# One layer of attention, RWKV mixing and two feed-forward blocks in float32: two scales moved to ScalarE, sums moved from VectorE to adding DMAs, one more sum begun in PSUM

## The reference, cut to what matters

```
x = x + attention(layernorm(x))          # (xn Wq^T)(xn^T xn), no softmax
x = x + ffn(layernorm(x))                # f1
x = rwkv(x):  x = x + time_mix(ln1(x));  x = x + channel_mix(ln2(x))
x = x + ffn(layernorm(x))                # f2, the same weights as f1

ffn(y):  z = y + relu(y W1 + b1) W2 + b2         # the router's weight is 1 for expert 0
         return (z - mean(z)) * rsqrt(var(z) + eps) * gamma + beta
```

## Time and profile before

| | |
|---|---|
| median of 3 runs | 262.93 us (262.4 to 263.28) |
| the profiled execution | 264.55 us |
| its span, first to last instruction | 262.8 us |
| TensorE busy | 253.0 us (96%) |
| VectorE busy | 232.7 us (89%) |
| ScalarE busy | 227.4 us (87%) |
| GpSimd busy | 153.1 us (58%) |

### The profile page before, as it was taken

One profiled execution on the slowest core, in us unless ns is written; L12 is line 12 of the kernel. 1 busy time (PEld: TensorE's weight loads), 2 busy tenths in 40 slices (PEclk: granted clock), 3 DMA queues, 4 the chain that ended last, 5 costly groups with the idle time before them and its releaser, 6 DMA issues.

```text
span 262.8 us, 5291 instructions
## 1 busy us (share of the span) xinstructions
PE 253.0 (96%) x1508; PEld 189.6 (72%) x1508; DVE 232.7 (89%) x762; ACT 227.4 (87%) x439; POOL 153.1 (58%) x290
## 2 busy tenths in 40 slices
PE   7999999999999999999999999999999999999991
PEld 6877686778777686667677767757874977777771
DVE  4598699999999999999999999999999987816384
ACT  1589899988988999899999999999999999993640
POOL 4558788832984774657927166964817158353522
PEclk9999999999999999999999999999999999999997
DMA  7922202402024220222403142063222526450332
GB/s 204 300 90 41 41 2 41 80 0 42 1 44 80 40 40 4 40 41 42 81 1 60 22 80 42 1 115 69 50 49 49 110 46 108 94 114 12 64 96 80
DMA packets 16908, 16.53 MB, mean 63 GB/s; under 512 B 1392, under 2 KB 11504, under 8 KB 16880
## 3 DMA queue, kind: packets, MB, share of 16 engines
q0 software_dynamic: 5616, 10.23, 22.9%
q1 hardware_dynamic: 10848, 5.84, 8.0%
q10 hardware_dynamic: 416, 0.14, 0.2%
HBM read 3.87 MB, written 2.10 MB: 23 GB/s over the span
## 4 chain that ended last, share of the span: by engine, by line
PE 84%; ACT 4%; POOL 4%; issue 3%; DVE 3%; DMA 1%; DVEq 0%; ACTq 0%; POOLq 0%
PE bank L1117 19%; PE bank L1126 19%; PE bank L1188 10%; PE bank L1194 8%; PE bank L1076 7%; PE bank L1089 3%; PE bank L1104 3%; PE bank L1169 3%; PE bank L1164 3%; PE bank L1205 2%; PE bank L1175 2%; PE bank L1159 2%; PE bank L1237 1%; DMA R<-in_hidden 1%; ACT f_h L907 1%
## 5 line engine op out<-in xcount | busy, mean ns | idle before, releaser
L1126 PEld LDWEIGHTS bank<-W,f_h 128*128 128x128 f32 x480 | 59.0, 192 | 12.0 <-issue 11.0
L1117 PE MATMUL bank<-f_yT,W 128*128 128x512 f32 x128 | 63.3, 595 | 0.0
L1126 PE MATMUL bank<-W,f_h 128*128 128x128 f32 x480 | 60.8, 275 | 0.0
L1194 PEld LDWEIGHTS bank<-FWv,KK 128*128 128x128 f32 x256 | 30.9, 192 | 3.4 <-issue 2.6
L1194 PE MATMUL bank<-FWv,KK 128*128 128x128 f32 x256 | 32.2, 276 | 0.0
L1188 PE MATMUL bank<-XK,FWk 128*128 128x512 f32 x64 | 30.5, 596 | 0.8 <-ACT KK L964 0.6
L1117 PEld LDWEIGHTS bank<-f_yT,W 128*128 128x128 f32 x128 | 21.2, 191 | 12.4 <-issue 7.8
L840 ACT ACTIVATE f_y<-R,f_yn_nb,f_yn_rs 128x128 f32<-128x128 f32 x64 | 26.3, 484 | 3.3 <-POOL f_yn_nb L350 3.1
L907 ACT ACTIVATE f_h<-bank,B1C 128x512 f32<-128x512 f32 x36 | 24.3, 686 | 0.2 <-PE bank L1126 0.2
L907 ACT ACTIVATE f_h<-bank,B 128x512 f32<-128x512 f32 x28 | 18.6, 681 | 6.0 <-PE bank L1126 3.3
L293 POOL TENSOR_TENSOR f_yn_ve<-f_yn_mv,K_EPS 128x4 f32<-128x4 f32 x16 | 7.3, 457 | 25.1 <-DVE f_yn_mv L529 25.1
(11 more groups left out here) (160 smaller groups left out, 637.2 us busy)
## 6 DMA issues: line engine op xcount, KB each, us to landing
R<-BETA POOLq DMA_DIRECT2D x16, 256.0 KB, 3.4
R<-f_zg POOLq DMA_DIRECT2D x11, 256.0 KB, 3.4
R<-N POOLq DMA_DIRECT2D x8, 256.0 KB, 3.7
R<-in_hidden SPq DMA_DIRECT2D x7, 256.0 KB, 5.6
out_x<-R SPq DMA_DIRECT2D x7, 256.0 KB, 2.3
R<-G POOLq DMA_DIRECT2D x4, 256.0 KB, 3.5
W<-in_w SPq DMA_DIRECT2D x2, 256.0 KB, 5.1
BETA<-in_beta SPq DMA_DIRECT2D x1, 256.0 KB, 5.2
```

What stands on the lines that cost most here:

```text
L1117: t_.matmul(banks[bank][:], W1[:, n * P:(n + 1) * P], at(f.yT, b)[:], start=True, stop=True).then_inc(f.h_psum[n], 1)
L1126: last = t_.matmul(banks[bank][:, j * C:(j + 1) * C], at(f.h, b)[:, n, j * P:(j + 1) * P], W2[:, n, :], start=False, stop=(n == H - 1), sk ...
L1194: last = t_.matmul(banks[bank][:, j * C:(j + 1) * C], at(KK, b)[:, n, j * P:(j + 1) * P], FWv[:, n, :], start=(n == 0 and j == 0), stop=(n ...
```

## The change

The change has four parts.

1. **First tile.** `first_shift` and `first_power` leave GpSimd. ScalarE does the same with a logarithm (bias eps) and an exponential (scale -0.5). TensorE now begins with `attn_transpose(0)`, whose first two parts read only the first half, and `attn_gram(0)` follows. `bias_rows` moves from behind `attn_proj(0)` to behind `attn_gram(2)`.
2. **Last tile.** `last_shift` and `last_power` become `last_log` and `last_root` on ScalarE, at the end of its list. `last_scaled(0)` moves ahead of `last_mean_var(0)`.
3. **Sums.** `ffn_add` is removed: the sums of `f1` tile 4 and of `f2` tiles 5 and 6 become `ffn_sum` on GpSimd. `cmix_out` stays for tile 7 alone: tiles 0, 1 and 6 become `cmix_sum`. `f2` tile 4 joins `STARTED`, so one `ffn_start` leaves TensorE and one comes to VectorE.
4. **Order and banks.** All four lists are written anew, with other banks. TensorE's has 127 calls with a wait for a bank where it had 135.

`z_log` and `z_root` are defined, and nothing calls them. The core of the diff (the lists are cut to their ends):

```diff
-ADDED = {"f1": (0, 4), "f2": (5, 6, 7), "x3": (0, 1, 6, 7)}
+ADDED = {"f1": (0,), "f2": (7,), "x3": (7,)}
 SPLIT = {"f1": (0,), "f2": (7,)}
-STARTED = {"f1": (0, 1, 2, 3), "f2": (5, 6, 7)}
+STARTED = {"f1": (0, 1, 2, 3), "f2": (4, 5, 6, 7)}
...
@@ gpsimd
-            first_shift(0); first_power(0); first_shift(1); first_power(1); shift(1, na); power(1, na); bias(1, na)
+            shift(1, na); power(1, na); bias(1, na); shift(2, na); power(2, na); bias(2, na); shift(3, na)
...
+            ffn_sum(4, f1, f1.zg); ffn_residual(5, f1); shift(1, ncm); power(1, ncm); back_scale(2); bias(1, ncm)
...
-            z_shift(6, f2); power(6, f2.znorm); last_shift(0); last_power(0); last_shift(1); last_power(1)
+            power(5, f2.znorm); ffn_residual(7, f2); ffn_sum(5, f2, f2.zg); z_shift(6, f2); power(6, f2.znorm)
+            ffn_sum(6, f2, f2.zg)
@@ vector
-            warm_tile(); first_stats(0); first_mean_var(0); first_stats(1); first_mean_var(1); attn_stats(1)
-            first_normed(0); first_normed(1); bias_diagonal(); mean_var(1, na); attn_stats(2); attn_stats(3)
+            warm_tile(); first_stats(0); first_mean_var(0); first_stats(1); first_mean_var(1); first_normed(0)
+            first_normed(1); attn_stats(1); mean_var(1, na); attn_stats(2); mean_var(2, na); attn_stats(3)
...
-            ffn_scaled(6, f2, 6); ffn_add(6, f2, f2.zg); last_stats(0, 5); last_mean_var(0); last_stats(1, 3)
-            last_mean_var(1); last_scaled(0, 5); last_scaled(1, 3); last_out(0); last_out(1)
+            ffn_scaled(5, f2, 1); z_stats(6, f2, 3); mean_var(6, f2.znorm); ffn_scaled(6, f2, 3); last_stats(0, 0)
+            last_scaled(0, 0); last_mean_var(0); last_stats(1, 2); last_mean_var(1); last_scaled(1, 2); last_out(0)
+            last_out(1)
@@ scalar
+            def log_rows(n, rows, wait, b, done):
+                act.wait_ge(*wait)
+                if b >= 2:
+                    act.wait_ge(f2.zg_ready, b - 1)
+                c = slice(rows[0], rows[-1] + 1)
+                a.activation(n.ve[b % 2][:, c], n.mv[b % 2][:, c, 1], ACT.Ln, bias=K_EPS[:, 0:1]).then_inc(done, 1)
+            def root_rows(n, rows, wait, b, done):
+                act.wait_ge(*wait)
+                c = slice(rows[0], rows[-1] + 1)
+                a.activation(n.rs[b % 2][:, c], n.ve[b % 2][:, c], ACT.Exp, scale=-0.5).then_inc(done, 1)
...
-            gram_evacuate(0, 0); attn_evacuate(0, 1); proj_evacuate(0, 0); attn_normed(1); attn_normed(2)
+            first_log(0); first_root(0); first_log(1); first_root(1); attn_evacuate(0, 0); gram_evacuate(0, 1)
+            proj_evacuate(0, 1); attn_normed(1); attn_normed(2); gram_evacuate(1, 2); attn_evacuate(1, 0)
+            attn_evacuate(2, 1); proj_evacuate(1, 2); attn_normed(3); gram_evacuate(2, 3); ffn_normed(0, f1)
...
-            relu(7, f2, 3, 1)
+            relu(7, f2, 3, 5); relu(7, f2, 2, 1); last_log(0); last_root(0); last_log(1); last_root(1)
@@ tensor
-            attn_gram(0, 0); attn_transpose(0, 1); attn_proj(0, 0); bias_rows(); attn_apply(0, 0)
-            attn_transpose(1, 1); attn_gram(1, 2); attn_transpose(2, 0, x1.ready(0)); attn_proj(1, 2); attn_gram(2, 3)
-            attn_proj(2, 3); attn_apply(1, 2); ffn_transpose(0, f1, 0); attn_apply(2, 3); hidden_up(0, f1, 2, 0)
+            attn_transpose(0, 0); attn_gram(0, 1); attn_proj(0, 1); attn_apply(0, 1); attn_transpose(1, 0)
+            attn_gram(1, 2); attn_transpose(2, 1, x1.ready(0)); attn_proj(1, 2); attn_gram(2, 3); bias_rows()
+            attn_apply(1, 2); attn_transpose(3, 1); attn_proj(2, 3); attn_gram(3, 4)
+            ffn_transpose(0, f1, 2, x1.ready(1)); attn_apply(2, 3); attn_proj(3, 7, b2_rows.done(0, "column"))
+            hidden_up(0, f1, 0, 2); hidden_up(0, f1, 2, 3, x1.ready(2)); hidden_up(0, f1, 3, 4)
...
-            hidden_up(7, f2, 2, 0, (f2.zg_ready, 6)); hidden_up(7, f2, 1, 2); hidden_up(7, f2, 3, 1)
-            last_down_first(0, 5, 3); last_down_first(1, 5, 3); last_down(0, 5); last_down(1, 3)
+            hidden_up(7, f2, 2, 1, (f2.zg_ready, 6)); hidden_up(7, f2, 0, 4); hidden_up(7, f2, 1, 7)
+            hidden_up(7, f2, 3, 5); last_down_first(0, 0, 2); last_down_first(1, 0, 2); last_down(0, 0)
+            last_down(1, 2)
```

More of the change, by code:

```diff
@@ L433, in _ @@
[L433 to L435 removed]
+            shift(1, na); power(1, na); bias(1, na); shift(2, na); power(2, na); bias(2, na); shift(3, na)
+            power(3, na); bias(3, na); shift(0, f1.norm); power(0, f1.norm); bias(0, f1.norm); shift(4, na)
@@ L1253, in _ @@
-            attn_gram(4, 6); hidden_up(2, f1, 1, 2); attn_transpose(4, 7, (xa_ready, 1)); hidden_up(2, f1, 0, 4)
-            product_k(0, 0); hidden_up(2, f1, 3, 2, (f1.h_ready[1], 3)); attn_gram(5, 6)
-            attn_proj(4, 3, (f1.zg_ready, 2)); ffn_transpose(3, f1, 7); attn_apply(4, 3)
-            hidden_up(2, f1, 2, 6, (gram_ready, 6)); attn_transpose(5, 7); product_v(0, 0, expo.done(0, "diff"))
-            product_r(0, 3, x1.ready(4)); ffn_down(2, f1, 0, 5); ffn_down(2, f1, 1, 5); ffn_down(2, f1, 2, 5)
@@ new lines, in _ @@
+            hidden_up(1, f1, 3, 0, (f1.zg_ready, 1)); hidden_up(1, f1, 2, 6); ffn_down(1, f1, 0, 3)
+            ffn_down(1, f1, 1, 3); ffn_down(1, f1, 2, 3); ffn_down(1, f1, 3, 3); attn_gram(4, 6)
+            tmix_transpose(0, 4, x1.ready(3)); attn_transpose(4, 0); hidden_up(2, f1, 3, 7)
+            hidden_up(2, f1, 1, 4, (xa_ready, 1)); hidden_up(2, f1, 2, 1); product_k(0, 2); attn_proj(4, 6)
+            hidden_up(2, f1, 0, 7, (f1.h_ready[3], 3)); attn_apply(4, 6); ffn_transpose(3, f1, 1, (f1.h_ready[2], 3))
@@ new lines, in _ @@
+            ffn_down(3, f1, 2, 2); attn_proj(5, 4, gate.done(0, "rl")); ffn_transpose(4, f1, 0); ffn_down(3, f1, 3, 2)
+            attn_apply(5, 4); attn_transpose(6, 0, (f1.yT_ready, 5)); product_o(0, 1)
+            hidden_up(4, f1, 1, 3, (b1_ready, 1)); attn_proj(6, 4, x1.ready(5)); ffn_start(4, f1, 0, (xnT_ready, 7))
+            hidden_up(4, f1, 0, 7); product_v(1, 6); attn_apply(6, 4); attn_transpose(7, 1, (u1_ready, 1))
+            hidden_up(4, f1, 2, 5); hidden_up(4, f1, 3, 3, (f1.h_ready[1], 5)); product_r(1, 4, x1.ready(6))
```

487 lines of the change are left out of this document (245 added, 242 removed).

## The result

The kernel after takes 260.74 us (median of 14 executions, 260.37 to 262.32); the kernel before, in turn with it on the same chips, takes 263.07 us (14 executions, 262.38 to 265.75). The ratio is 0.991, with a 95% interval of 0.988 to 0.994: faster by 2.3 us. The prediction said 261.2 us, between 258.6 and 263.8. The profiled execution of after took 260.81 us, its span is 259.0 us.

The account below looks back on a forecast made before the run. TensorE was taken as bound: 242.6 us of work, about 7.5 us not work, some 5.5 of it waits beside full VectorE and ScalarE. Terms -0.8 - 0.45 - 0.5 + 0 = -1.75 from 262.93 gave 261.2 us, range 258.6 to 263.8.

Parts of the forecast that it names:

- Last tile: After TensorE's last product: VectorE is the path, nothing to gain; 0 taken, between -0.15 and +0.3 us.
- One `ffn_start` less: On TensorE, the path that sets the end: four instructions of 0.11 us go, -0.45 us.
- First tile: At the start: norming and TensorE's first real work come earlier; -0.8 us taken, between -1.2 and -0.3.
- Sums to DMAs: Six adds leave VectorE, three where it is full; fewer TensorE waits, -0.5 us, between -4 and +2.5.
- a quarter of 2.0 us: In the full middle: VectorE's 2.0 us relief counted at a quarter, as ScalarE is equally full: -0.5 us.
- The waits go: TensorE throughout: VectorE gets ahead, 4 of the 5.5 us of waits vanish, 258.2 us; chance 0.15.
- Nothing comes of it: Full middle engines can't follow TensorE's lead at 20 us; at most 0.45 us stays, 262.7 us; chance 0.16.
- A sum lands late: GpSimd's queue delays a sum's issue; two VectorE stalls of 1.3 to 1.5 us, 264.4 us; chance 0.13.
- the covers that the prediction counted: VectorE calls between a sum's issue and its use, worth 4.8 to 7.9 us, hide the DMA's 3.4 us landing.
- The clock rises later: TensorE's start: transposes first may not raise the clock; 1.7 us more at the lower level, 262.1 us; chance 0.06.

Follow-up runs that it names:

- e2: Kernel before with the last tile's scales on ScalarE and the first half's gain product ahead of its aggregates on VectorE: 262.22 us against 262.98, ratio 0.997.
- e9: Kernel before with only the last tile's two scales moved to ScalarE, VectorE's order as it was: 262.34 us against 263.37, ratio 0.997.
- e10: Kernel before with only VectorE's last-tile order changed (first half's gain product moved ahead), scales kept on GpSimd: 263.1 us against 263.37, ratio 0.999.
- e6: Kernel after with the `ffn_start` of tile 4 of `f2` (four transposes) back on TensorE: 262.36 us, ratio 0.994 to the kernel before.
- E3: Kernel after with the first tile's two scales back on GpSimd, transposes still first: 261.75 us, ratio 0.995 to the kernel before.
- e1: Kernel before with the first tile's scales on ScalarE, transposes first, `attn_stats(1)` behind `first_normed`: 262.79 us against 262.98, ratio 0.999.
- e5: Kernel after with six sums back on VectorE, each right behind its factor: 264.32 us against 264.35 for the kernel before, ratio 1.001.
- e7: Kernel after with first and last scales on GpSimd, six sums on VectorE, `f2` tile 4 started on TensorE: 266.4 us against 264.35 before, ratio 1.010.

## Why the prediction was right, step by step

The time was 0.5 us under the one named. One of the four terms was 1.0 us too small, two were 0.2 us too large.

**Last tile: 0 taken, 1.0 us measured.** This is the step that failed. The prediction said that `last_scaled(0)` ahead of `last_mean_var(0)` would push the second half's statistics back by 0.25 us. They are not pushed back: they start 0.89 us behind the first half's in before (256.42 and 257.31) and in after (253.67 and 254.56), and in both 0.04 us after the end of the last 16 products (257.27 and 254.52). They have to wait for the bank of the second half anyway, and the gain product fills this gap. That is 0.33 us (e2 against e9), and it needs ScalarE's scale (e10). The other 0.6 us is a place where the prediction didn't look: behind the last output. Where GpSimd works on the last tile, SyncE waits 0.8 us for the closing rendezvous, otherwise 0.2. What GpSimd does in this time the trace doesn't show. SyncE's store of tile 6 was no danger: it is issued at 255.12, 1.1 us ahead of the first half's.

**One `ffn_start` less: 0.45 us.** Not contradicted, and not measured by itself: e6 lost 0.8 to 1.6 us, by the way it is counted, with another thing in it that is worth some 1.05.

**First tile: 0.8 us taken, about 0.6 measured.** The prices were right (0.29 and 0.20 against 0.28 and 0.19; start at 5.81 against about 6). E3 gives 0.6 us for the scales. The lead against the profile of before looks like 2 us (0.47 at `hidden_up` plus 1.55 of work done), but 1.3 to 1.4 us of this are the late rise of the clock in that execution. Against e2 and e9, where `hidden_up` stands at 17.50 and 17.36, after is 0.8 to 1.0 us behind with 1.55 us more done: 0.6 to 0.7 ahead. The prediction had `hidden_up` at 19.9, with the same 14 instructions done; its time by hand was 1.6 us too late, and 1.2 to 1.4 of that stand already behind the first twelve instructions (8.5 to 8.7 against 7.34), which it priced at the lower level. It counted on a sooner rise of the clock for up to 0.7 us. Nine of the 14 executions of before lie in the group that by the table has no late rise, so a sooner rise could not move the median by 0.7 us, and that the 0.8 us came out near the measured 0.6 is in part luck. That GpSimd's scale of tile 1 takes back part of the lead was right: this is where e1 loses it.

**Sums to DMAs: 0.5 us taken, about 0.3 measured,** as the sum of two large numbers. VectorE's busy time fell by 2.0 us to 230.7, where the prediction had 229.3; the seven instructions concerned are worth about what it counted (4.0 us of adds gone, 0.7 of `ffn_start` come), but the busy time counts what overlaps once. The new order without the sums on DMAs (e5) is 2.7 to 3.3 us slower than with them, and the order with nothing else (e7) is 2.5 to 3.5 us slower than before. So "a quarter of 2.0 us" gave about the right net by a way that isn't the chip's. What the six adds are worth by themselves in a list made for them can't be told from here: no run had the old order with sums on DMAs, and e5 puts each add at a place that nobody chose.

The terms as measured: 1.0 + 0.45 + 0.6 + 0.3 = 2.35 us, against 2.33 us between the medians. Each is known to some tenths only, and 0.45 is not measured, so that they meet this well is partly luck.

**The rivals.** *The waits go*: no; TensorE's busy time from 100 to 140 us rose from 38.96 to 40.00 us, and from 20 to 60 it fell from 39.98 to 39.28, so one wait was exchanged for another. *Nothing comes of it*: no. In the old order the head's change by itself does give nothing (e1), but not for the reason that this rival named. Full engines do keep a lead at 20 us: e2 is 1.29 us ahead of before at `hidden_up` and 1.27 at the last products. The head's lead is lost before 20 us, at tile 1. *A sum lands late*: the waits view of VectorE in after has one wait for an adding DMA between 20 us and the end:

```profile
DVE tmix_stats L447 <- DMA R<-f_zg: 0.3, 1, 0.3
```

It is 0.3 us, far under the 1.3 to 1.5 that the rival asked for; the covers that the prediction counted held. *The clock rises later*: no. In after, the four transposes that come first are 0.12 us apart and the products behind them 0.11, so the upper level was there at 5.81 us. That doesn't contradict the rule of the Trainium skill, "TensorE: Matmul & The Clock Gate", "Part 4: PE-mode transpose": the warm-up ahead of them are products, and the level may have risen by these. In e1 the first four, at 5.61, take 1.00 us, because the second two wait for the second half's `XN`; the eight behind them take 1.06. Whether transposes help to raise the clock no run here shows.

## What to carry to other kernels

An engine that is out of the way in the last microseconds shortens the program's closing rendezvous: look at the waits behind the last output too, and give the last small steps to an engine that ends early anyway. A lead that stands when the full middle of a pipeline begins is there at its end, but a faster first step is worth nothing where the second tile's scale is the next thing waited for: look at where the lead ends before pricing it. An order is worth less than nothing without the change it was made for; so undo parts within the new order before putting a price on one. Before two profiles are compared, see to which group of times each belongs. When the executions of a kernel fall into groups, compare two profiles of different groups row by row: one prolonged instruction can be found in this way.
